# Stream 1's scratch and first chunks through ScalarE's queue, its gathers earlier, and TensorE matmuls without a reader at the start

## What is computed

```
e = stack(tbl_f[ids[:, f]] for f in 0..31)                  # (1024, 32, 16)
xk = x0 = e
for W in (W0, W1, W2):                                      # 64 maps each
    xk = relu(einsum('bmd,bhd,mhk->bkd', x0, xk, W))
    outs.append(sum(xk, axis=2))
h = concatenate(outs + [dense_ctx], axis=1)                 # (1024, 208)
h = maximum(h @ W_top1 + b_top1, 0)
h = maximum(h @ W_top2 + b_top2, 0)
y = h @ W_top3
```

## Time and profile before

| | us |
|---|---|
| median of 3 runs | 616.87 (615.1 to 616.98) |
| the profiled execution's own time | 617.09 |
| its span, first to last instruction | 615.3 |
| mean granted clock of TensorE | 0.994 of full |
| TensorE busy | 562.9 (91%) |
| VectorE busy | 553.3 (90%) |
| POOL busy | 451.6 (73%) |
| ScalarE busy | 366.7 (60%) |

### The profile page before, as it was taken

The page is one execution under the profiler, slowest core; times in us unless marked ns, Lnnn a source line. Parts: engine busy times, 40 slices in busy tenths (PEclk is TensorE's granted clock), DMA queues, the critical chain, the costliest instruction groups (busy, mean ns, idle before and its releaser), DMA issues.

```text
span 615.3 us, 9070 instructions
## 1 busy us (share of the span) xinstructions
PE 562.9 (91%) x2752; PEld 209.7 (34%) x2752; DVE 553.3 (90%) x274; ACT 366.7 (60%) x2248; POOL 451.6 (73%) x347
## 2 busy tenths in 40 slices
PE   0049889999999999999999999999999999999997
PEld 0012222323333343334333333334333343334334
DVE  0058799999999999999999999999999999999990
ACT  0031606573867468774867468774868468674851
POOL 6748788878888788888888788888878864225430
PEclk9998899999999999999999999999999999999999
DMA  6297969793598819894598819794598809891000
GB/s 171 78 381 247 395 224 393 257 399 111 184 387 289 325 36 385 293 399 136 180 390 276 334 39 382 277 400 154 181 390 321 320 6 388 294 411 49 1 2 0
DMA packets 54259, 152.07 MB, mean 247 GB/s; under 512 B 9697, under 2 KB 18913, under 8 KB 54210
## 3 DMA queue, kind: packets, MB, share of 16 engines
q1 hardware_dynamic: 46018, 149.39, 64.6%
q0 software_dynamic: 8192, 2.11, 3.0%
HBM read 147.26 MB, written 4.20 MB: 246 GB/s over the span
## 4 chain that ended last, share of the span: by engine, by line
PE 74%; DVE 10%; DMA 6%; issue 4%; POOL 3%; SPq 1%; ACT 1%; DVEq 0%; POOLq 0%
PE acc L591 66%; DVE zd L413 10%; DMA rolled<-x_scratch 4%; POOL emb L330 3%; PE mlp L635 2%; PE acc L600 2%; PE mlp L626 1%; DMA emb<-tables_in,index 1%; PE mlp L627 1%; SPq L294 1%; DMA x_scratch<-emb 1%; PE mlp L607 1%; PE mlp L642 1%; ACT xk_sb L481 0%; ACT xk_ps L481 0%
## 5 line engine op out<-in xcount | busy, mean ns | idle before, releaser
L413 DVE TENSOR_TENSOR zd<-rolled,xk_ps 128x2048 f32<-128x2048 f32 (+1 forms) x246 | 536.1, 2254 | 11.6 <-DMA rolled<-x_scratch 5.3
L591 PE MATMUL acc<-zd,w_sb 128*64 128x512 f32 x1700 | 389.2, 596 | 8.9 <-DVE zd L413 8.8
L330 POOL DMA_INDIRECT emb<-tables_in,index x256 | 244.3, 954 | 79.6 <-issue 65.3
L342 POOL TENSOR_TENSOR zg<-rolled,xk_sb 128x1024 f32<-128x1024 f32 x87 | 207.1, 2383 | 59.3 <-ACT xk_sb L481 36.9
L591 PEld LDWEIGHTS acc<-zd,w_sb 128*64 128x64 f32 x1700 | 124.8, 137 | 250.2 <-issue 213.9
L460 ACT ACTIVATE relu_ab<-acc 128x16 f32<-128x16 f32 x928 | 153.7, 305 | 3.7 <-PE acc L591 3.5
L460 ACT ACTIVATION_READ_ACCUMULATOR relu_ab<-acc 128x1 f32 x928 | 154.3, 332 | 0.0
L481 ACT ACTIVATE xk_sb<-acc 64x512 f32<-64x512 f32 x128 | 75.8, 592 | 70.1 <-PE acc L591 67.5
L591 PE MATMUL acc<-zd,w 128*64 128x512 f32 x256 | 63.7, 618 | 38.6 <-DVE zd L413 38.6
L591 PE MATMUL acc<-zg,w_sb 128*64 128x512 f32 x348 | 90.7, 594 | 1.4 <-POOL zg L342 1.4
L481 ACT ACTIVATE xk_ps<-acc 64x512 f32<-64x512 f32 x126 | 71.8, 570 | 30.4 <-PE acc L591 27.6
(11 more groups left out here) (45 smaller groups left out, 102.5 us busy)
## 6 DMA issues: line engine op xcount, KB each, us to landing
rolled<-x_scratch SPq DMA_DIRECT2D x256, 512.0 KB, 10.3
base<-x_scratch SPq DMA_DIRECT2D x16, 512.0 KB, 3.7
emb<-tables_in,index POOLq DMA_INDIRECT x256
x_scratch<-emb SPq DMA_DIRECT2D x32, 128.0 KB
w_sb<-w_in SPq DMA_DIRECT2D x2, 512.0 KB, 5.0
wt<-wtop_in SPq DMA_DIRECT2D x1, 512.0 KB, 6.9
wt1a<-wtop_in SPq DMA_DIRECT2D x1, 256.0 KB, 5.8
w<-w0a_in SPq DMA_DIRECT2D x1, 160.0 KB, 2.3
```

The lines of the kernel that those rows point to most:

```text
L330: pool.indirect_dma_start(emb[:, i % 2, c * DIM:(c + 1) * DIM], None, tables, bass.IndirectOffsetOnAxis(index[:, g:g + 1].bitcast(U32), 0) ...
L342: nc.gpsimd.tensor_tensor(zg[:, n % ZG_BUFS, :], rolled[:, s, j, :], xk_sb[:, s, :], ALU.mult).then_inc(zg_ready, 1)
L413: nc.vector.tensor_tensor(zd[:, n % ZD_BUFS, 0:w, :], rolled[:, s, j:j + w, :], repeated(layer_in, w), ALU.mult).then_inc(zd_ready, 1)
L591: end = nc.tensor.matmul(acc[h * MAPS:(h + 1) * MAPS, bank, :], weights, z[:, h * HALF:(h + 1) * HALF], start=(j + c == 0), stop=(i == len ...
```

## The change

Four things are done.

1. `GATHERS_FIRST` goes from 24 to 28 and `GATHERS_EARLY` from 8 to 4, so four more gathers are issued before POOL's wait for phase (0,0,0). The gathers behind the products of the first phases are put otherwise: (0,1,0) from 4, 7 to 3, 2; (0,2,0) from 3 to 8; (1,1,0) from 3, 4 to 5, 6; (0,2,1) from 7 to 8.
2. Stream 1's store to scratch, its `base` and its chunks 0 to 3 are issued by ScalarE, behind `evacuate(0, 0)`. SP keeps chunks 4 to 15 of stream 1, behind a wait for the scratch alone; all other streams stay with SP.
3. Phase (0,0,0)'s four products go into four halves of `zd`, none of them waiting for `zd_used`; the next phase waits for its buffers as before.
4. TensorE issues 20 matmuls 128x128 into `mlp`, which nobody reads, when stream 0's scratch is stored, and 14 more between phases (0,0,0) and (0,1,0).

```diff
+WARM_BEFORE = 20
+WARM_BETWEEN = 14
...
-GATHERS_FIRST = 24
-GATHERS_EARLY = 8
+GATHERS_FIRST = 28
+GATHERS_EARLY = 4
...
-GATHERS_AFTER_AT = {(0, 1, 0): [4, 7], (0, 2, 0): [3], (1, 1, 0): [3, 4], (0, 2, 1): [7],
+GATHERS_AFTER_AT = {(0, 1, 0): [3, 2], (0, 2, 0): [8], (1, 1, 0): [5, 6], (0, 2, 1): [8],
...
+        def zd_of(q, n, w):
+
+            return zd[:, n // 2, n % 2:n % 2 + 1, :] if q == 0 else zd[:, n % ZD_BUFS, 0:w, :]
...
+        def load_chunk(engine, i, j):
+            engine.dma_start(rolled[:, i % 2, j, :], rows_from(BASES[j], i, 1)).then_inc(rolled_in[i % 2][j], 16)
...
-                if i > 0:
-
-                    if i == 1:
-                        sp.wait_ge(zd_ready, len(PLAN.dve[0]))
-                    else:
-                        sp.wait_ge(base_ps, 2 * (i - 1))
+                if i > 1:
+
+                    sp.wait_ge(base_ps, 2 * (i - 1))
                     sp.wait_ge(squares_ready, i)
-                sp.dma_start(base[:, :], rows_from(0, i, 0)).then_inc(base_in, 16)
+                if i != 1:
+                    sp.dma_start(base[:, :], rows_from(0, i, 0)).then_inc(base_in, 16)
...
-                        sp.dma_start(rolled[:, s, j, :], rows_from(BASES[j], i, 1)).then_inc(rolled_in[s][j], 16)
+                        if i != 1 or j >= L0CH:
+                            load_chunk(sp, i, j)
...
-                store_scratch(i)
+                if i != 1:
+                    store_scratch(sp, i)
                 load_stream(i)
...
-                    if n >= ZD_BUFS:
+                    if q > 0:
 
                         dve.wait_ge(zd_used, n - ZD_BUFS + 1)
...
             evacuate(0, 0)
+
+            store_scratch(act, 1)
+            act.wait_ge(scratch_in[1], 32)
+
+            act.wait_ge(zd_ready, len(PLAN.dve[0]))
+            act.dma_start(base[:, :], rows_from(0, 1, 0)).then_inc(base_in, 16)
+            for j in range(L0CH):
+                load_chunk(act, 1, j)
             base_to_ps(1)
...
-            for q in range(6):
+            def keep_clock_up(n):
+
+                for _ in range(n):
+                    nc.tensor.matmul(mlp[:, 0:TB], eye_sb[:, :], wt1a[:, 0:TB], start=True, stop=True)
+
+
+            pe.wait_ge(scratch_in[0], 32)
+            keep_clock_up(WARM_BEFORE)
+            phase(0)
+
+            keep_clock_up(WARM_BETWEEN)
+            for q in range(1, 6):
                 phase(q)
```

More of the change, by code:

```diff
@@ L259, in build_cin_tower, with rows_from, store_scratch @@
         last_y_bank = xk_ps[0:1, 0, 0:TB]
+        def rows_from(first, i, step):
+            return bass.AP(scratch.tensor, scratch.offset + (i * ROWS + first) * COLS,
+                           [[COLS, FIELDS], [step * COLS, GROUPS], [1, COLS]])
+        def store_scratch(engine, i):
+            engine.wait_ge(gathered[i % 2], 16 * GATHERS * (i // 2 + 1))
+            for copy in range(2):
+                engine.dma_start(scratch[i, copy * FIELDS:(copy + 1) * FIELDS, :].rearrange(
+                    "f (g c) -> (f g) c", g=GROUPS), emb[:, i % 2, :]).then_inc(scratch_in[i % 2], 16)
+        def load_chunk(engine, i, j):
+            engine.dma_start(rolled[:, i % 2, j, :], rows_from(BASES[j], i, 1)).then_inc(rolled_in[i % 2][j], 16)
         @block.sync
         def _(sp):
[L263 to L272, removed]
-            def load_stream(i):
-                s = i % 2
-                sp.wait_ge(scratch_in[s], 32 * (i // 2 + 1))
-                if i > 0:
-                    if i == 1:
-                        sp.wait_ge(zd_ready, len(PLAN.dve[0]))
-                    else:
-                        sp.wait_ge(base_ps, 2 * (i - 1))
+            def load_stream(i):
+                sp.wait_ge(scratch_in[i % 2], 32 * (i // 2 + 1))
+                if i > 1:
+                    sp.wait_ge(base_ps, 2 * (i - 1))
                     sp.wait_ge(squares_ready, i)
-                sp.dma_start(base[:, :], rows_from(0, i, 0)).then_inc(base_in, 16)
+                if i != 1:
+                    sp.dma_start(base[:, :], rows_from(0, i, 0)).then_inc(base_in, 16)
                 user = (i - 2, 2) if i > 1 else (i, 1)
@@ L412, in _ @@
                     layer_in = base[:, :] if q == 0 else xk_ps[:, s, :]
-                    nc.vector.tensor_tensor(zd[:, n % ZD_BUFS, 0:w, :], rolled[:, s, j:j + w, :],
+                    nc.vector.tensor_tensor(zd_of(q, n, w), rolled[:, s, j:j + w, :],
                                             repeated(layer_in, w), ALU.mult).then_inc(zd_ready, 1)
@@ L588, in phase @@
                         weights = w0[:, j + c, :] if layer == 0 else w12_sb[:, layer - 1, j + c, :]
-                        z = zd[:, n % ZD_BUFS, c, :] if who == "dve" else zg[:, n % ZG_BUFS, :]
+                        z = zd_of(q, n, w)[:, c, :] if who == "dve" else zg[:, n % ZG_BUFS, :]
                         for h in range(2):
```

## The result

| | before | change |
|---|---|---|
| time, median | 616.43 us (5 runs, 614.52 to 616.98) | 625.37 us (5 runs, 625.05 to 626.42) |
| profiled execution: own time / span | 617.09 / 615.3 us | 626.42 / 624.5 us |
| mean granted clock of TensorE | 0.994 | 0.992 |

The ratio is 1.0142 (95% interval 1.0113 to 1.0172): the change makes the kernel slower by 9 us. The prediction said 616.7, from 613.7 to 619.3. The result lies outside this range, and above what its slower rival said too (619.1 to 621.3).

A forecast was written before the change was run, and what follows sets the result against it. TensorE was taken to bound the middle, so the start of (1,1,0) on VectorE would set the end: -0.35 us there, 0 for POOL's gathers, on 617.09 gave 616.7 us, range 613.7 to 619.3.

The forecast's parts named there:

- From there on four gathers more are done than before, which holds up nobody.: POOL after tile 0's moved gathers: four more gathers already done than before, at no cost to any engine.
- a loss or a gain of the start is carried to the end unchanged: Middle 73 us, TensorE busy for all 73.00: only its work counts there, so start shifts reach the end in full.
- T: Issue of stream 1's base: 51.0 us, 4.6 earlier than 55.63; at the least 49.5, at the most 53.3.
- The turns of the queues: Stream 1's loads: ScalarE's and SP's queues alternate, so chunk 3 lands at T + 16.4, 67.4 us, 0.95 later than before.
- Rival B: Start: stream 1's store waits for stream 0's loads; (1,1,0) at 79.25 or later, total 619.1 to 621.3 us; chance 0.18.
- The matmuls: Phase (0,0,0): unread matmuls raise TensorE's clock, so VectorE's (0,1,0) starts 2.0 us earlier, at 41.45.
- D: Phase (0,0,0): unread matmuls don't raise the clock, (0,1,0) still starts at 43.5; end 0.7 us late (617.8); chance 0.07.
- GpSimd's row in tile 0: POOL's products: (1,2,0) starts at 104.95 instead of 99.28, TensorE waits 1.5 us for it and catches up; cost 0.
- The sum: Whole kernel: -0.35 us on the profiled execution's 617.09 gives 616.7 us.

## Why the prediction was wrong, step by step

**The step that failed: "From there on four gathers more are done than before, which holds up nobody."** I had asked what a late product costs, and not what an early gather meets. What stands in its way is the wait at the head of each stream, for a buffer that SP's store frees. Instead of nothing, the four gathers cost 5.2 to 5.6 us in the change, and 6.5 to 7.6 alone. The view that I had read (a 73 us stretch in the middle without idle time on TensorE) was right, but "a loss or a gain of the start is carried to the end unchanged" doesn't follow from it: GpSimd has no room in a tile either (62.31 of 73 us busy, and the 0.30 us of issue between its gathers on top). The row that would have told me was in the trace of before: at 462.39 a gather waits 3.62 us for the scratch (shown above). GpSimd was at this limit already. This step alone doesn't account for the miss: without the four gathers the change is at 620.19 us, which is still above the range, by the next step.

**T, the moment at which base is issued, was mis-sized:** 51.0, measured 54.82. Three terms. The last gather went out at 43.72 for 42.84: POOL waits for VectorE's fourth product before its last four gathers (it stood idle for 1.00 us before 39.97), and that product came 0.9 us later than before (38.47 for 37.60). It landed 6.1 us later (49.81), not 4.0. The store took 5.0 us, not 4.1. The 2.58 came from a quiet DMA, and here it was full to 52. The 4.0 was a gather's under full traffic too; why this one took 6.1 isn't shown. In no run without a stall did stream 1's last gather take less than 5.1; it was 6.0 to 6.1 in all five that had it early together with the matmuls, and 5.3 to 5.4 in the three that had it early without them. Over these runs the store went out anywhere from 48.3 to 53.05, and base only from 53.7 to 55.6. That fits a T set by the end of stream 0's loads, which no run moved. Even the upper bound of T (53.3, "when the loads are over and a store takes its quiet time") was 1.5 us too low; worked out by its own words, from loads that end at 51.8 and a store of 2.58, it is 54.4.

**The turns of the queues were right.** T + 16.4 and T + 11 for chunks 3 and 1, measured T + 16.25 and T + 11.13; base at T + 5.4, measured T + 5.56. Holding SP back takes the turns away and the time with them (chunk 3 at T + 9.9). The Trainium skill's rule on turns between queues (DMA: Bandwidth & Descriptors, Queues, rings and completion order) agrees with all of these. For the store I can't say so: why 0.26 MB in a second queue should take until the first one's loads end isn't shown.

**Rival B was right about the start**, with its formula: T + 25.95 gives 80.8 for (1,1,0), measured 80.46. But its T was 53.3 to 55.6 for a start at 79.25 and later, and its cost ends at the start; of the four gathers it says nothing. Without the four gathers the change is at 620.19, inside its 619.1 to 621.3. It had a chance of 0.18 only, because I gave weight to one gather (4.0 us) and not to the last one of stream 1 (5.2), which stood nearer to the place.

**The matmuls:** the clock rose, as forecast, for the first phase (units of 0.86 us; the granted clock is 1.00 from 36 to 40 us). (0,1,0) starts at 42.35, not 41.45, since the last chunk of stream 0 was multiplied 0.9 us later (38.47 for 37.60). What they won was swallowed by the wait for chunk 1, and alone they bring nothing: right. D is refuted.

**GpSimd's row in tile 0:** product (1,2,0) was forecast at 104.95 and came at 108.54, 3.6 late. 2.9 of these stand already at the product of (0,2,0) (64.89 for 62.0): base's landing at 60.38 held the evacuation that it waits for, as the prediction had said of a late base. The other 0.7 is a wait for xk_sb before the next product (0.80 us, at 77.92). TensorE waited 1.37 us (forecast 1.5), and it cost nothing there: 3.2 us late at (1,1,0), 3.2 at 154.95. Right.

**The sum** was -0.35; with T as measured it would have been about +3.5, and with the 5.2 to 5.6 of the four gathers about +9.

## What to carry to other kernels

A wait at the head of a buffer ring limits how far ahead an engine may run, and an engine that does other work behind that wait passes it on: before moving work forward on an engine that is nearly full, look in the steady stretch for the waits that already stand at this ring, even small ones that cost nothing yet. Compare the totals at the end of the moved piece (60 gathers here, 64 there): one number of a table was worth 5 to 8 us. And a transfer put into a second queue shares with the first one: here the loads that were wanted first stayed first only when the others were held.

## What the runs showed that I had not expected

- **A stall of 8 to 12 us with the same text.** Three of the four kernels measured first, on one chip, lost 8 to 12 us in TensorE's first phase; two of them, loaded again on another chip, lost nothing (627.45 and 620.19 us; 632.24 and 624.57). By the times it is in all runs of a load (626.61 to 628.16). In two of the three TensorE's records trickle in by ones with "issue" before each, while the DMA is full (share 1.02 to 1.03 from 32 to 48 us); in the one without matmuls they are complete at 40.83, and ScalarE and VectorE start on them at 48.59. Of the queue that the profile calls instruction, one packet (q8) lay at 42 to 46 us in the change and in the undisturbed load, and at 54 to 58 in the disturbed one. The Trainium skill (Runtime: NRT & Kernel Launch, Instruction fetch mechanics) says that an engine's instructions come in blocks of 16 KiB through a DMA queue of its own, and that this is mostly hidden. That a block held up by the loads is the cause would fit, but in the pair without matmuls the packet lay after 66 us in both loads, so it isn't shown; load and chip aren't told apart either. What follows: one text measured in one load can be 1.2% off for all of its runs, and the profile of that load shows it.
- **Some gathers near 35 us take longer to issue:** 1.83 us at 34.42 and 1.15 at 37.81 in the change, instead of 0.94. The same place has none in the change with four gathers fewer, loaded again (0.94 to 0.95 from 32.99 to 36.73), and later gathers take 0.94 to 0.99 while VectorE is busy without a gap. What stretches them isn't shown.
- **A gather under full traffic took 6.1 us to land** in the change, and 4.0 and 5.2 in the kernel before (those of 173.38 and 47.83).
